# First expert loop: the second block's rows picked by one-hot products

## The reference, cut to what matters

```python
logits = x @ gate_w + gate_b                       # 625 x 8
topk_vals, topk_idx = top_k(logits, 2)
topk_weights = softmax(topk_vals)
weights = einsum('bske,bsk->bse', one_hot(topk_idx, 8), topk_weights)
h = relu(einsum('bsh,ehf->bsef', x, w1) + b1)      # 512 -> 1024, per expert
expert_out = einsum('bsef,efh->bseh', h, w2) + b2  # 1024 -> 512
return einsum('bseh,bse->bsh', expert_out, weights)
```

## Time and profile before

| | |
|---|---|
| median of 3 runs | 1784.19 us (1782.05 to 1787.66) |
| the profiled execution, its own time | 1787.7 us |
| its span, first to last instruction | 1785.9 us |
| TensorE busy | 1567.6 us, 88% |
| VectorE busy | 1240.9 us, 69% |
| ScalarE busy | 938.1 us, 53% |
| GpSimd busy | 247.8 us, 14% |
| mean granted clock of TensorE | 0.932 of 2.4 GHz |

### The profile page before, as it was taken

The page is one execution under the profiler, slowest core; times in us unless marked ns, Lnnn a source line. Parts: engine busy times, 40 slices in busy tenths (PEclk is TensorE's granted clock), DMA queues, the critical chain, the costliest instruction groups (busy, mean ns, idle before and its releaser), DMA issues. The chain is left out here.

```text
span 1785.9 us, 25655 instructions
## 1 busy us (share of the span) xinstructions
PE 1567.6 (88%) x8459; PEld 1249.5 (70%) x8459; DVE 1240.9 (69%) x2031; ACT 938.1 (53%) x1590; POOL 247.8 (14%) x250
## 2 busy tenths in 40 slices
PE   7778899998998899657999958598779999999998
PEld 6657666686785678436878846385568888888886
DVE  7873665246463546467999975544569999999998
ACT  1122345433461356115989935242148778778774
POOL 2200453001120012015000030100063000000003
PEclk9878799999999899968999989699889999999999
DMA  9001000003100000305594140000426507956003
GB/s 302 28 0 48 1 1 1 12 1 131 48 1 24 13 1 32 123 31 168 186 343 150 50 159 1 1 0 5 208 64 236 212 35 297 366 241 235 18 19 97
DMA packets 42460, 173.56 MB, mean 97 GB/s; under 512 B 10219, under 2 KB 10472, under 8 KB 26905
## 3 DMA queue, kind: packets, MB, share of 16 engines
q1 hardware_dynamic: 28822, 153.94, 23.0%
q0 software_dynamic: 8960, 10.29, 2.1%
q10 hardware_dynamic: 4608, 8.39, 1.2%
HBM read 275.74 MB, written 19.51 MB: 165 GB/s over the span
## 5 line engine op out<-in xcount | busy, mean ns | idle before, releaser
L654 POOL DMA_INDIRECT sb_W<-slots_out,sb_slus x20 | 28.2, 1411 | 612.1 <-DMA slots_out<-sb_rC 606.6
L1856 DVE COPY sb_rA<-bank 125x625 f32<-125x625 f32 (+4 forms) x60 | 43.3, 722 | 72.1 <-PE bank L833 72.1
L357 DVE TENSOR_TENSOR sb_rA_r<-sb_W,sb_rA_r 128x1024 fp32r<-128x1024 f32 x68 | 83.2, 1224 | 12.6 <-ACT sb_rA_r L1449 12.6
L603 POOL TENSOR_TENSOR sb_rstd<-sb_ve,sb_half 125x5 f32<-125x5 f32 (+1 forms) x17 | 18.9, 1114 | 517.6 <-DVE sb_ve L1769 245.1
L725 PE MATMUL bank<-sb_ident,sb_XN 125*128 125x125 f32 x160 | 30.2, 373 | 69.0 <-DVE sb_XN L1795 69.0
L833 PE MATMUL bank<-sb_ident,sb_rF 125*125 125x125 f32 x520 | 85.0, 289 | 6.1 <-DVE sb_rA L1856 2.8
L1351 ACT ACTIVATE sb_rF<-sb_rF,sb_nmx 125x625 f32<-125x625 f32 (+4 forms) x120 | 88.3, 738 | 1.6 <-DVE sb_nmx L1847 1.4
L1847 DVE CUSTOM_DVE_ANT_0 sb_rF<-bank,sb_rG 125x625 f32<-125x625 f32 x80 | 61.5, 806 | 35.6 <-PE bank L820 35.1
L833 PEld LDWEIGHTS bank<-sb_ident,sb_rF 125*125 125x125 f32 x520 | 65.8, 187 | 26.9 <-issue 17.2
L1102 PE MATMUL bank<-sb_rA 125*125 125x313 bf16 x400 | 65.1, 331 | 21.9 <-DVE sb_rA L2168 18.7
L357 DVE TENSOR_TENSOR sb_rB_r<-sb_W,sb_rB_r 128x1024 fp32r<-128x1024 f32 x68 | 82.8, 1217 | 0.0
(11 more groups left out here) (496 smaller groups left out, 4850.0 us busy)
## 6 DMA issues: line engine op xcount, KB each, us to landing
sb_W<-in_w_m SPq DMA_DIRECT2D x204, 1024.0 KB
sb_rDE<-in_w_m SPq DMA_DIRECT2D x17, 1024.0 KB
sb_rC<-slots_in SPq DMA_DIRECT2D x34, 256.0 KB, 2.7
sb_W<-in_w_g SPq DMA_DIRECT2D x8, 1024.0 KB, 4.8
slots_out<-sb_rC ACTq DMA_DIRECT2D x32, 256.0 KB, 2.0
slots_in<-sb_rC SPq DMA_DIRECT2D x1, 4608.0 KB, 14.5
sb_W<-in_w_a SPq DMA_DIRECT2D x4, 1024.0 KB, 31.0
sb_W<-in_w_m SPq DMA_DIRECT2D x2, 2048.0 KB, 18.8
```

The costliest lines, as they stand in the source:

```text
L357: eng.tensor_tensor(lo, src[:, HALF * h:HALF * (h + 1)], hi.bitcast(F32), ALU.subtract).then_inc(split(r, p, h, b, "lo")[0], 1)
L654: pool.indirect_dma_start(out=G[r][k][:, t], out_offset=None, in_=YS[0:P * KEPT], in_offset=bass.IndirectOffsetOnAxis(ap=slus[:, k, t:t + ...
L1856: dve.tensor_copy(PT[:, u % 4, 0:nb, :], pt).then_inc(S("at_pt"), 1)
```

## The change

The one-hot products that bring together block 0 are done for block 1 too. VectorE subtracts 128 from the slots (`sl1`) and makes five tiles `SEL1[t]` in parts of `rA` and `rB` that nothing uses at that time (`second_rows`, between `blocks_of` and `second_biases`). TensorE multiplies by them (`chosen_nodes`) after first("a", 1, 0) and before turn(0, 0); nodes(1) of TensorE and SyncE's read of block 1 go away. The scatters stay, for all rows. The semaphores `ld_a0_0` to `ld_a0_3` and `ld_g0` to `ld_g3` become four shared ones, `ld_p0` to `ld_p3`, with counts to match, and the counts of `ld_xb` follow the missing read. In the second expert loop nothing is changed but these counts.

```diff
--- before.py
+++ after.py
@@ -187,6 +187,7 @@
         sls = sb("sls", [R, 2, T])
         slr = sb("slr", [R, 2, T])
         slus = sb("slus", [R, 2, T], U32)
+        sl1 = sb("sl1", [R, 2, T])
         eb = sb("eb", [P, 2, BLOCKS])
         ebi = sb("ebi", [1, 2, BLOCKS], I32)
         red = sb("red", [R, 3, T])
@@ -309,7 +310,8 @@
 
 
         SEL0 = W[0:R, 16384:16384 + T * P].rearrange("p (t n) -> p t n", t=T)
-        L0 = {1: 0, 3: BLOCKS}
+        SEL1 = [rA[0:R, 4 * D + t * P:4 * D + (t + 1) * P] if t < 4 else rB[0:R, 4 * D:4 * D + P] for t in range(T)]
+        L0 = {1: -1, 3: BLOCKS - 1}
         ST0 = {1: 0, 3: KEPT}
         B0, X0, C0 = {1: 0, 3: BLOCKS}, {1: 0, 3: BLOCKS + 1}, {1: 0, 3: BLOCKS * CH[1]}
 
@@ -438,7 +440,7 @@
                     if after_first:
                         sp.wait_ge(S(names[i]), layer * counts[i])
                     sp.dma_start(W[:, 4096 + 2048 * i:6144 + 2048 * i],
-                                 A["w_g"][layer, :, i]).then_inc(S(f"ld_g{i}"), 16)
+                                 A["w_g"][layer, :, i]).then_inc(S(f"ld_p{i}"), 16)
                 if after_first:
                     sp.wait_ge(S("g_w2_full"), layer * 8)
                 sp.dma_start(W[:, 16384:17408], A["w_gf"][layer]).then_inc(S("ld_gf"), 16)
@@ -494,7 +496,6 @@
                 weights(("a", 0), 1, e, new)
                 weights(("a", 1), 1, e, new)
                 sp.wait_ge(S("sc"), 16 * 2 * T * (r // 2 + 1))
-                nodes(1)
                 nodes(2)
                 weights(("y", 0), 1, e, new)
                 with sp.Fori(2, BLOCKS) as b:
@@ -523,7 +524,7 @@
             sp.dma_start(rbias[:], A["rbias"].to_broadcast([P, RBW])).then_inc(S("ld_small"), 16)
             sp.dma_start(b2[:], A["b2"][0]).then_inc(S("ld_b2"), 16)
             for i in range(4):
-                sp.dma_start(W[:, 4096 + 2048 * i:6144 + 2048 * i], A["w_a0"][:, i]).then_inc(S(f"ld_a0_{i}"), 16)
+                sp.dma_start(W[:, 4096 + 2048 * i:6144 + 2048 * i], A["w_a0"][:, i]).then_inc(S(f"ld_p{i}"), 16)
             sp.dma_start(W[:, 12288:16384].rearrange("p (e n) -> p e n", e=4),
                          A["w_m0"][0:4].rearrange("e p n -> p e n")).then_inc(S("ld_m0a"), 16)
             sp.wait_ge(S("h_full"), 8)
@@ -1023,12 +1024,11 @@
                     product(("y", j), b, bank[:, 7, :], [hTh[:, j % 2, i * P:(i + 1) * P] for i in range(4)],
                             [hTl[:, j % 2, i * P:(i + 1) * P] for i in range(4)], j == 0, j == n - 1)
 
-                def first_nodes():
-
-                    pe.wait_ge(S("sl_vec"), SLOT_OPS * (r // 2) + SELECTED)
+                def chosen_nodes(chosen):
+
                     for k in range(C):
                         for t in range(T):
-                            mm = pe.matmul(bank[:, 6, k * P:(k + 1) * P], XN[:, t, k * P:(k + 1) * P], SEL0[:, t],
+                            mm = pe.matmul(bank[:, 6, k * P:(k + 1) * P], XN[:, t, k * P:(k + 1) * P], chosen(t),
                                            start=(t == 0), stop=(t == T - 1))
                     mm.then_inc(S("b_xt"), 1)
 
@@ -1050,9 +1050,11 @@
                     else:
                         second_biases(2, T)
                         first("a", 1, b)
+                        pe.wait_ge(S("next_rows"), T)
+                        pe.wait_ge(S("b_xbl"), 1)
+                        chosen_nodes(lambda t: SEL1[t])
                         pe.wait_ge(S("b2_done"), T)
                         turn(0, b)
-                        nodes(b + 1)
                     if before is not None:
                         second(1, before)
 
@@ -1072,7 +1074,8 @@
                         second(j - 1, b)
 
                 body = body1 if r == 1 else body3
-                first_nodes()
+                pe.wait_ge(S("sl_vec"), SLOT_OPS * (r // 2) + SELECTED)
+                chosen_nodes(lambda t: SEL0[:, t])
                 body(0, None)
                 body(1, 0)
                 with pe.Fori(2, BLOCKS) as b:
@@ -1198,7 +1201,7 @@
                 heads(3 + t, t, 2, LOW_LAST, True, True)
             attention(lambda k: 0, True, lambda: pe.wait_ge(S("kvq_done"), 3 * T))
             pe.wait_ge(S("at_norm"), NORM * T)
-            pe.wait_ge(S("ld_a0_3"), 16)
+            pe.wait_ge(S("ld_p3"), 16)
             project([(Wo, OT)], S("wo0_full"))
             pe.wait_ge(S("ld_small"), 48)
             for c in range(C):
@@ -1215,7 +1218,7 @@
             ln_to_feats(3)
             feats_ready(4)
             for layer in range(LAYERS):
-                pe.wait_ge(S("ld_g0"), layer * 16 + 16)
+                pe.wait_ge(S("ld_p0"), layer * 16 + 32)
                 project([(Wq, XT[:])], S("g_q_full"))
                 Wk2, Wv2 = ([w[i].rearrange("p (c n) -> p c n", c=C) for w in (gw_hi, gw_lo)] for i in range(2))
                 pe.wait_ge(S("mx_hi"), layer * C + (SX + 3 * C))
@@ -1234,7 +1237,7 @@
                 row_group_split(7, gx, 4, Wv2, S("g_v_full"))
                 attention(lambda k: layer * k + k, False, lambda: pe.wait_ge(S("g_v_done"), layer * 5 + 5))
                 pe.wait_ge(S("at_norm"), layer * (NORM * T) + 2 * NORM * T)
-                pe.wait_ge(S("ld_g3"), layer * 16 + 16)
+                pe.wait_ge(S("ld_p3"), layer * 16 + 32)
                 project([(Wo, OT)], S("g_wo_full"))
                 pe.wait_ge(S("ld_gf"), layer * 16 + 16)
                 for i, (lo, hi) in enumerate(HALVES):
@@ -1589,7 +1592,7 @@
             bn_apply(HB, HB, ACT.Relu, S("bn_vec"), 16, S("bn_out"))
 
             def weights_high(i):
-                act.wait_ge(S(f"ld_a0_{i}"), 16)
+                act.wait_ge(S(f"ld_p{i}"), 16)
                 act.activation(qw[i][0], (Wq, Wk, Wv)[i], ACT.Copy).then_inc(S("mw_hi"), 1)
 
             weights_high(0)
@@ -1652,7 +1655,7 @@
                             act.activation(gx[0][:, c], XT[:, c], ACT.Copy).then_inc(S("mx_hi"), 1)
                     elif j in (2, 4):
                         i = j // 2 - 1
-                        act.wait_ge(S(f"ld_g{i + 1}"), layer * 16 + 16)
+                        act.wait_ge(S(f"ld_p{i + 1}"), layer * 16 + 32)
                         act.activation(gw_hi[i], (Wk, Wv)[i].rearrange("p c n -> p (c n)"), ACT.Copy).then_inc(S("mw_hi"), 1)
                 def values(t, b):
                     act.wait_ge(S("g_v_full"), layer * 5 + t + 1)
@@ -1990,6 +1993,17 @@
                     c(dve.tensor_reduce(biases, bprod, AX.X, ALU.add))
                     c.sync()
 
+            def second_rows():
+
+                dve.tensor_scalar(sl1[:], sl[:], float(P), None, ALU.subtract).then_inc(S("rows_off"), 1)
+                dve.wait_ge(S("rows_off"), 1)
+                for t in range(T):
+                    dve.tensor_scalar(SEL1[t], iotaP[0:R], sl1[:, 0, t:t + 1], None, ALU.is_equal).then_inc(S("rows_off"), 1)
+                for t in range(T):
+                    dve.wait_ge(S("rows_off"), t + 2)
+                    dve.scalar_tensor_tensor(out=SEL1[t], in0=iotaP[0:R], scalar=sl1[:, 1, t:t + 1], in1=SEL1[t],
+                                             op0=ALU.is_equal, op1=ALU.add).then_inc(S("next_rows"), 1)
+
             def second_biases():
 
                 c = Chain(dve, S("b2_done"))
@@ -2039,6 +2053,7 @@
                     lows(("a", 1), b)
                     if before is None:
                         blocks_of(1)
+                        second_rows()
                         second_biases()
                     hidden(0, b)
                     if before is not None:
```

## The result

The changed kernel takes 1777.35 us, median of 20 runs (1774.9 to 1783.96); the kernel before, 20 runs beside it, 1780.09 us (1778.96 to 1787.66). The ratio is 0.9984, 95% interval 0.9976 to 0.9992: faster by 2.8 us, between 1.4 and 4.3, which is less than the 0.3% (5.35 us) that the forecast took as the bound of "no change". The forecast gain was 2.6 us.

The account below looks back on a forecast made before the run. TensorE was taken to set the loop, VectorE hardly behind, with a loose pause from 820 to 830. Earlier rows 2.19 us plus clock 0.4 made 2.6 us; 1784.19 - 2.6 = 1781.6 us, range 1778.8 to 1786.0.

Parts of the forecast that it names:

- the base: The whole kernel's time before the change, taken as a median of 1784.19 us, from which 2.6 us was subtracted.
- rival 5: Block 1's start: weights come earlier and the clock stays up, gaining 4.6 us, to 1779.6 us; chance 0.07.
- the 0.4 us of the clock: TensorE in block 1: a shorter pause may keep 2.4 GHz, worth 0 to 0.8 us, middle taken.
- rows that come earlier are worth 2.19 us, and no more unless the weights come earlier too: Block 1's start: xbh on ScalarE begins at 826.4, behind the weight copies, instead of 828.59.
- Tiles 2.81 us: VectorE behind blocks_of: one subtraction, ten comparison operations and two gaps take 2.81 us.
- Products 4.4 us at 1.00: TensorE: block 1's 20 products, 40 recorded instructions, take 4.4 us at 2.4 GHz.
- Start at 820.32: TensorE's products for block 1 wait for VectorE's tiles and start at about 820.32.
- The cover of 5.40 us, of which 0.4 is left: VectorE's idle time before block 1's xbh covers the 2.81 us; 0.4 us remains with the earlier xbh.
- VectorE lost at most 0.17 us on such an operation: VectorE beside GpSimd: five comparisons with an add lose at most 0.85 us in all; taken as 0.
- rival 2: GpSimd's L643 holds up VectorE's five comparisons with an add: 1785.6 us, or 1790.8 if stretched; chance 0.08.
- Tiles allocated after sl1 stand 40 bytes further on ... nothing: Later tiles in each partition: the shifted address changes no time, since L357 takes 1,216 ns or 1.22 us.
- what block 1 gains at its start should stay gained: First expert loop: TensorE sets it, with VectorE hardly behind, so the gain at block 1 should persist.

Follow-up runs that it names:

- experiment 1: The kernel before, run again beside itself with no edit: 1780.03 us against 1780.54, ratio 0.9995.
- Experiment 4: The changed kernel with block 1's 20 products computed a second time, with the same result: 1783.38 us, ratio 1.0014 to the kernel before.
- Experiment 3: The changed kernel, but nobody reads VectorE's tiles and block 1 is read from the table as before: 1779.0 us, ratio 0.9994 to the kernel before.
- Experiment 9: On top of experiment 8, ScalarE and VectorE do what doesn't need block 1's rows ahead of them: 1775.83 us, ratio 0.9967 to the kernel before.
- Experiment 7: The changed kernel with GpSimd's preparation in the first loop begun eight b_xt later: 1776.51 us, ratio 0.9981 to the kernel before.
- experiment 8: The changed kernel with blocks_of and second_rows moved ahead of block 0's xbl on VectorE: 1776.32 us, ratio 0.9984 to the kernel before.
- 10: Experiment 9 with GpSimd's comparison tiles held back until block 8: 1776.59 us, ratio 0.9976 to the kernel before.
- experiment 6: The changed kernel with sl1 allocated behind all other tiles, so none is moved: 1777.88 us, ratio 0.9995 to the kernel before.

## Why the forecast was right in its gain and wrong in its time

**The term that failed is the base**: "so for a median: 1784.19 - 2.6". 1784.19 was the middle of three runs (1782.05, 1784.19, 1787.66). The median of 20 is 1780.09, and experiment 1 gives 1780.0 again. The base was 4.1 us too high, which is more than the whole effect. 1780.09 - 2.6 would have been 1777.5. The profiled execution could have warned: its 1787.7 was 3.5 us above even that median, and, as experiment 1 shows, 7.3 us of it had been lost ahead of the mark. The range took in "half" of the spread of 5.6 us about the forecast; but three runs of which the profiled one is the highest say little of where the middle of many lies, and a lower end near 1776 was called for. The same half of the spread about rival 5's 1779.6 would have reached 1776.8.

**That the gain came out near is in part luck.** Block 1's start gained 2.5 to 2.9 us, more than the 2.19 forecast, in the first profiles since the weights landed earlier; the 0.4 us of the clock was in blocks 1 and 2 together not there; and the profiles have 4.0 us from the mark to the end where the timed medians have 2.8. Ahead of the mark the twelve profiles differ by almost 9 us (it stands from 788.85 to 797.68), so the 1.2 us between the two can't be assigned.

**Point by point.**
- *"rows that come earlier are worth 2.19 us, and no more unless the weights come earlier too"*: right about the rows. In the first profiles xbh moved from 828.59 - 797.53 = 31.06 to 28.19 us from the mark, 2.87 us. The 0.7 above 2.19 are the weights, which landed at 26.28 instead of 26.86 us, and xbh overlapping the end of the copy. Experiment 4 shows the gate, with 0.8 us of slack. But "unless the weights come earlier too" left out VectorE: in the changed kernel's second profile they did, and the first product came no earlier. By the forecast's own numbers VectorE's low halves, done at 826.63, allowed a gain of at most 829.22 - 826.63 = 2.6 us, so rival 5's 3.84 us was not to be had.
- *Tiles 2.81 us*: 2.74. *Products 4.4 us at 1.00*: 4.74 at 1.00, from 817.82 to 822.56. *Start at 820.32*, 22.79 us from the mark: 22.77.
- *The cover of 5.40 us, of which 0.4 is left*: the cover was there, but nothing of it is left (823.83 against an xbh that ends at 823.82), since xbh came earlier than forecast. Experiment 3 shows that the tiles without the rest cost at most 0.8 us.
- *The clock, 0.4 out of 0 to 0.8 us*: the level did stay up, and block 1 took 13.46 us instead of 14.03. But block 2 took 13.06 instead of 12.40, so nothing was kept: behind TensorE stood VectorE's low halves. Experiment 9 moved them ahead, and the two blocks took 24.9 us instead of 26.5.
- *"VectorE lost at most 0.17 us on such an operation"*: too low as a bound for all its operations. Beside the ten comparisons it holds (2.74 and 2.80 us against 2.6 with GpSimd quiet), so rival 2 fell. But the additions L647, which the forecast didn't look at, now ran beside block 1, where operations of 1.22 us took 1.48. Experiment 7 prices GpSimd's work there at 0.8 us in blocks 1 and 2. By the rule of the Trainium skill ("SBUF — State Buffer", Who interferes with whom) the second to issue waits until the first is done. The trace goes with it for GpSimd, whose additions come about one per low half (1.25 us each), and only in part for VectorE, which loses 1.48 - 1.22 = 0.26 us where a whole addition is recorded with 0.45; for which part of the 0.45 the addition reads SBUF isn't seen.
- *"Tiles allocated after sl1 stand 40 bytes further on ... nothing"*: wrong in both loops and nearly nothing in sum: 0.03 to 0.04 us lost in each steady block of the first loop, at most some 0.6 us in its 16, and 469.4 - 468.9, some 0.5 us, gained behind the start of the last. The rows used as evidence compared two outputs, while `W`, which both read, was moved in any case.
- *"what block 1 gains at its start should stay gained"*: only roughly. From the mark to the last loop, all twelve profiles (two of either kernel and eight of others) give 515.5, 518.9 or 522.3 to 522.4 us and nothing between, though the first loop ends anywhere from 242.3 to 251.5. Loops that ended up to 245.9 gave 515.5, 247.2 to 249.1 gave 518.9, and 249.4 and more 522.3. The changed kernel gained 2.5 to 2.9 us at block 1 and 3.4 at the last loop; experiment 8 gained 1.2 more and kept none of it.

The differences shrink on the way and are gone before the last loop's own products start. Of the seven profiles that start it at 515.5, the first loop ends spread over 3.6 us (242.3 to 245.9). Some 26 us later, at L802 (L801 in before), the first products behind the gates' L742, 1.4 us are left (269.0 to 270.4); at 416 us it is 0.5, and at 515.5 it is 0.06. TensorE's timeline shows how, for experiment 8 and then for experiment 9:

```profile
1049.52 4.43 PE L726 MATMUL bank<-sb_ident,sb_XN 125*128 125x125 f32 x20 [15.34 <-DVE sb_XN L1798]
1054.72 4.40 PE L742 MATMUL bank<-sb_XT,sb_gw 128*32 128x375 f32 x16 [0.77 <-DVE sb_XT L1751]
1059.05 3.72 PE L802 MATMUL bank<-sb_W,sb_XT 128*125 128x256 f32 x16
```

```profile
1047.68 4.43 PE L726 MATMUL bank<-sb_ident,sb_XN 125*128 125x125 f32 x20 [15.56 <-DVE sb_XN L1803]
1052.88 6.44 PE L742 MATMUL bank<-sb_XT,sb_gw 128*32 128x375 f32 x16 [0.77 <-DVE sb_XT L1756]
1059.25 3.72 PE L802 MATMUL bank<-sb_W,sb_XT 128*125 128x256 f32 x16
```

(L726 are transposes behind the loop, L742 the gates' products.) Counted from the marks, experiment 9 comes to L742 at 1052.88 - 789.20 = 263.68, and experiment 8 at 1054.72 - 790.04 = 264.68: a lead of 1.00. Then the same products take 6.44 us instead of 4.40, and the lead is a lag of 1.04. The single microseconds of TensorE in experiment 9 (busy time, granted clock, DMA share, GB/s) say why:

```profile
1053.00:1054.00 1.00, 1.00 (x2) 0.50 1.01 406
...
1056.00:1057.00 1.00, 1.00 (x3) 0.50 0.27 102
1057.00:1058.00 1.00, 1.00 (x5) 0.98 0.05 20
```

The level, low since TensorE had idled behind the loop, rises only at 1057.0, 267.8 us from the mark, and four of these microseconds of L742 run at 1.2 GHz. In experiment 8 the mean of the microsecond from 1054 is 0.75 and the next is 1.00: a rise at 1054.5, 264.5 from the mark, before L742 starts. Worked out in this way from the mean of the microsecond in which it falls, the rise is at 264.4 or 264.5 in the changed kernel's two profiles and experiment 8, and at 267.8 or 267.9 in experiments 9 and 10 and the first profile of before. It doesn't come earlier by as much as the work does: who comes before it works at 1.2 GHz until it is there. So a stretch that ends 1.4 us earlier than in experiment 8 (242.3 against 243.7) can end up no further ahead. The three places at which the last loop starts are tied to such a rise, too. Here are the single microseconds of TensorE around it, first in the changed kernel and then in experiment 6:

```profile
1308.00:1309.00 1.00, 1.00 (x8) 0.68 0.56 117
...
1311.00:1312.00 1.00, 1.00 (x9) 0.86 0.52 131
```

Worked out as above, the level rises at 1308.6 and 1311.3, 513.6 us from either mark, in the middle of the products (L1031) that pick the rows of the last loop's block 0. In all twelve profiles such a rise stands 1.8 to 1.9 us ahead of the last loop's start: at 513.6 where it is 515.5, at 517.0 where it is 518.9, at 520.4 where it is 522.3 or 522.4.

All this is read from traces: no experiment of its own holds the level and shows the gain kept. What puts a rise where it falls, and so why there are just three places, stays open.

## What to carry to other kernels

Ask first how far a few runs pin the base (here the gain was forecast to 0.2 us and the time missed by 4), and count from a mark just ahead of the change, which takes away what varies before it. When a read is taken off the path, list what stands next behind it on each engine and who works in the idle time that is about to close: here ScalarE's weight copies stood 0.8 us behind the products and VectorE's low halves at the same place, so that earlier weights alone gained nothing. And follow a small gain through every later stretch that begins at the lower clock, since it can be lost there without any new wait.

## What was not expected of the hardware

- Forty bytes in the place of the large tiles change the pace of a steady loop by 0.3% up (12.41 to 12.45 us) in one and 0.1% down (26.68 to 26.65 us) in another. Which operation in the block pays was not found.
- A low half on VectorE and an addition on GpSimd, each with two inputs in SBUF, slow each other very unequally: 1.22 to 1.48 us on VectorE, 0.45 to 1.25 us on GpSimd.
- The first 180 us of the program can make 7 us of difference between executions of the same kernel. Against the first profile of before, the second is 3.2 us earlier at 60 us, 6.7 at 120 us and 7.3 from 190 us on, and stays there up to the mark. Why was not tried.
